# Window attention on one core: x in eight window-column transfers a block, weights loaded ahead of the statistics

## What is computed

```python
# x: (8, 56, 88, 192) float32; windows of 7 x 11 = 77 tokens, 8 heads of 24 channels
def _L0_conv_ref(x, qkv_w, qkv_b, proj_w, proj_b):
    xw = windows(x)                                   # (B*8*8, 77, 192)
    q, k, v = split(xw @ qkv_w + qkv_b, 3)            # per head 24 channels
    attn = softmax(einsum('bhnd,bhmd->bhnm', q, k) / sqrt(24))
    out = einsum('bhnm,bhmd->bhnd', attn, v)
    return unwindow(out @ proj_w + proj_b)
# _gn: group norm over (H, W, channels of a group), 32 groups of 6 channels, per image
x = x + _L0_conv_ref(_gn(x), qkv_w, qkv_b, proj_w, proj_b)
```

## Time and profile before

| | |
|---|---|
| median of three runs | 1518.98 us (1517.67 to 1539.47) |
| the profiled execution | 1531.71 us, span 1529.9 us |
| TensorE | 1361.8 us busy, 89% of the span |
| granted TensorE clock, mean | 0.971 |
| VectorE, ScalarE, GpSimd | 68%, 67%, 64% |
| DMA | 170.36 MB, mean 111 GB/s |

### The profile page before, as it was taken

The page is one execution under the profiler, slowest core; times in us unless marked ns, Lnnn a source line. Parts: engine busy times, 40 slices in busy tenths (PEclk is TensorE's granted clock), DMA queues, the critical chain, the costliest instruction groups (busy, mean ns, idle before and its releaser), DMA issues.

```text
span 1529.9 us, 84594 instructions
## 1 busy us (share of the span) xinstructions
PE 1361.8 (89%) x36832; PEld 1210.0 (79%) x36832; DVE 1047.8 (68%) x2227; ACT 1025.4 (67%) x1912; POOL 977.4 (64%) x1532
## 2 busy tenths in 40 slices
PE   0489899999998999999999989998999989999995
PEld 0377788888887888888888878887888878888884
DVE  5677677677766766777667866777667766666662
ACT  1567677766776677776767766776667666767761
POOL 0546766677665766767667776777667576767433
PEclk9999999999999999999999999999999999999997
DMA  7233344444444444444444443544433333433333
GB/s 211 69 95 88 112 114 129 120 118 124 108 128 100 115 129 104 129 107 132 111 114 134 113 108 108 132 123 116 116 99 97 98 95 89 106 95 93 85 84 105
DMA packets 129892, 170.36 MB, mean 111 GB/s; under 512 B 46898, under 2 KB 101490, under 8 KB 128628
## 3 DMA queue, kind: packets, MB, share of 16 engines
q1 hardware_dynamic: 98292, 100.59, 26.8%
q10 hardware_dynamic: 31232, 64.35, 14.0%
HBM read 132.04 MB, written 31.54 MB: 107 GB/s over the span
## 4 chain that ended last, share of the span: by engine, by line
PE 77%; DVE 8%; issue 6%; ACT 3%; POOL 3%; DMA 2%; SPq 1%; ACTq 0%; POOLq 0%; DVEq 0%
PE ps_a L698 13%; PE ps_b L698 13%; PE ps_q L698 11%; PE ps_k L698 11%; PE ps_a L731 10%; PE ps_s L744 8%; PE ps_s L758 5%; PE ps_k L826 4%; PE ps_q L793 3%; DVE neg_max L632 2%; POOL st_root L336 2%; DVE stat L495 2%; ACT probs L469 1%; DMA bias_in<-in_qkv_b 1%; DVE st_dev L510 1%
## 5 line engine op out<-in xcount | busy, mean ns | idle before, releaser
L632 DVE TENSOR_REDUCE neg_max<-ps_s 77x16 bf16<-77x1232 f32 x256 | 369.6, 1444 | 221.9 <-PE ps_s L758 221.1
L371 POOL TENSOR_TENSOR oT_lo<-o,oT_hi 128x308 f16<-128x308 f32 x256 | 193.7, 756 | 321.1 <-ACT oT_hi L463 321.1
L469 ACT ACTIVATE probs<-ps_s,exp_shift,exp_scale 77x1232 f32<-77x1232 f32 x256 | 349.2, 1364 | 9.9 <-PE ps_s L744 9.1
L731 PE MATMUL ps_a<-probs,v_all 77*32 77x77 f32 x8192 | 200.6, 234 | 41.1 <-issue 39.8
L452 ACT ACTIVATE v_all<-ps_a 77x384 f32<-77x384 f32 x256 | 124.9, 488 | 166.5 <-PE ps_a L698 166.4
L698 PE MATMUL ps_a<-wv_hiA,xT 128*128 128x192 f16 x1024 | 218.7, 253 | 2.5 <-issue 1.8
L345 POOL TENSOR_TENSOR o<-num,inv_all 128x308 f32<-128x308 f32 x256 | 216.2, 845 | 4.7 <-DMA inv_all<-den_dram 4.7
L439 ACT ACTIVATE xT<-ps_k 128x448 f16<-128x448 f16 x347 | 209.5, 642 | 8.9 <-PE ps_k L826 8.9
L731 PEld LDWEIGHTS ps_a<-probs,v_all 77*32 77x32 f32 x8192 | 148.7, 110 | 68.8 <-issue 44.4
L698 PE MATMUL ps_b<-wp_hi,oT_hi 128*112 128x192 f16 x694 | 188.1, 271 | 13.0 <-POOL oT_lo L371 6.8
L433 ACT ACTIVATE num<-ps_a 128x308 f32<-128x308 f32 x256 | 109.3, 427 | 133.0 <-PE ps_a L731 118.6
(11 more groups left out here) (148 smaller groups left out, 3854.9 us busy)
## 6 DMA issues: line engine op xcount, KB each, us to landing
inv_all<-den_dram SPq DMA_DIRECT2D x1024, 38.5 KB
x_stat<-in_x SPq DMA_DIRECT2D x24, 504.0 KB, 6.1
x_norm<-in_x ACTq DMA_DIRECT2D x32, 336.0 KB
x_norm<-in_x ACTq DMA_DIRECT2D x64, 168.0 KB
y_blk<-in_x SPq DMA_DIRECT2D x32, 336.0 KB
y_blk<-in_x SPq DMA_DIRECT2D x64, 168.0 KB
out<-y_blk ACTq DMA_DIRECT2D x32, 336.0 KB
out<-y_blk ACTq DMA_DIRECT2D x64, 168.0 KB
```

What stands on the lines that cost most here:

```text
L371: nc.gpsimd.tensor_tensor(oT_tokens(oT_lo, o), by_column(o32[o % 2]), oT_tokens(oT_hi, o), ALU.subtract).then_inc(pool_oT, 1)
L469: nc.scalar.activation(probs[i % 2][:, :, :].rearrange("p g (a n) -> p g a n", a=4), scores(), ACT.Exp, bias=exp_shift[0:TOK, :], scale=ex ...
L632: nc.vector.tensor_reduce(neg_max[:, :, :, HD:HD + 1].rearrange("p a g e -> p g (a e)"), scores(), AXIS.X, ALU.max, negate=True).then_inc( ...
L731: last = mm(o, v_all[s % V_BUFS][:, HEADS * w + NG * j + g, :], probs[s % 2][:, g, at:at + TOK], start=True, stop=True, skip_group_check=True)
```

## The change

x is loaded by window column: a block has eight transfers, each of 14 partitions by one contiguous row of 11 x 192 floats (8448 B), all eight on one semaphore per buffer. In the loop two are issued in each of the slots i with i + 19 = 8c + r, r = 0 to 3 (slots 5, 6, 7 and 0); before, one piece in each of slots 6, 0, 2, 4. A load of block c now waits for GpSimd to have split all of block c - 2. GpSimd waits once a block for all eight, and for block 1 it waits also for VectorE's third `normalise`.

In the prologue SP issues the two bias rows first, then proj_w, and bp last. ScalarE issues the first statistics half, waits for the six transfers of `dma_rows`, issues the second half and block 0, and issues block 1 only after its conversion of the weights. The pieces of y and of the output stay.

```diff
@@ semaphores
-        dma_x = [[sem(f"dma_x{p}_{k}") for k in range(len(PIECES))] for p in range(2)]
+        dma_x = [sem(f"dma_x{p}") for p in range(2)]
@@ SP
-            sp.dma_start(bp[:, :], proj_b.rearrange("(a c) -> a c", a=1).broadcast_to([128, CH])).then_inc(dma_w, 16)
             sp.wait_ge(pool_const, 2)
+            b_row = qkv_b.rearrange("(a c) -> a c", a=1)
+            for row in (CB, CB + ROW_G):
+                sp.dma_start(bias_in[row:row + 1, :], b_row).then_inc(dma_rows, 16)
             p_rows = proj_w.rearrange("(j g d) c -> g d j c", g=NG, d=HD)
             for g in range(NG):
                 sp.dma_start(p32[ROW_G * g:ROW_G * g + HD, :, :], p_rows[g, :, :, :]).then_inc(dma_rows, 16)
-            b_row = qkv_b.rearrange("(a c) -> a c", a=1)
-            for row in (CB, CB + ROW_G):
-                sp.dma_start(bias_in[row:row + 1, :], b_row).then_inc(dma_rows, 16)
+            sp.dma_start(bp[:, :], proj_b.rearrange("(a c) -> a c", a=1).broadcast_to([128, CH])).then_inc(dma_w, 16)
@@ GpSimd
-                    if n % PAIRS_IMG == 0 or n == PAIRS:
+                    if n == PAIRS:
+                        pool.wait_ge(dve_norm0, 3)
+                    if n % PAIRS_IMG == 0:
                         pool.wait_ge(stats_done, g + 1)
-                    if n % 2 == 0:
-                        pool.wait_ge(dma_x[parity(n)][n % PAIRS // 2], 16 * (n // PAIRS // 2 + 1))
+                    if n % PAIRS == 0:
+                        pool.wait_ge(dma_x[parity(n)], NWC * 16 * (n // PAIRS // 2 + 1))
@@ ScalarE
-            def load_x(c, k):
+            def load_x(c, w):
                 if c == 2:
-                    act.wait_ge(dve_x0, 2 * k + 2)
-                reach(act, pool_x, PAIRS * (c - 3) + 2 * k + 2)
-                nc.scalar.dma_start(piece(x_norm[c % 2], k), piece_of(x_blk, c, k)).then_inc(dma_x[c % 2][k], 16)
+                    act.wait_ge(dve_x0, PAIRS)
+                reach(act, pool_x, PAIRS * (c - 2))
+                nc.scalar.dma_start(x_norm[c % 2][ROWS * w:ROWS * (w + 1), :, :].rearrange("p c d -> p (c d)"), x_blk[c, w, :, :])\
+                    .then_inc(dma_x[c % 2], 16)
+
+            def load_block(c):
+                for w in range(NWC):
+                    load_x(c, w)
@@ ScalarE, prologue
             for h in range(2):
+                if h == 1:
+                    act.wait_ge(dma_rows, 6 * 16)
                 for n in range(2):
                     nc.scalar.dma_start(x_stat[h][:, n * TILES:(n + 1) * TILES, :].rearrange("p c d -> p (c d)"),
                                         x_rows[2 * h + n, :, :]).then_inc(dma_stat[h], 16)
-            for c in range(2):
-                for k in range(len(PIECES)):
-                    load_x(c, k)
+            load_block(0)
@@ ScalarE, behind the weight conversion
             nc.scalar.activation(wv["Bb"][low, :], bias_in[low, v], ACT.Copy).then_inc(act_w, 1)
+            load_block(1)
             act.wait_ge(stat_var, 1)
@@ ScalarE, main loop
-                c, r = divmod(i + 18, PAIRS)
-                if r % 2 == 0 and 2 <= c < BLOCKS:
-                    load_x(c, r // 2)
+                c, r = divmod(i + 19, PAIRS)
+                if r < 4 and 2 <= c < BLOCKS:
+                    load_x(c, 2 * r)
+                    load_x(c, 2 * r + 1)
@@ VectorE
-            dve.wait_ge(dma_x[0][0], 16)
+            dve.wait_ge(dma_x[0], NWC * 16)
             normalise(1, 0, 4)
-            dve.wait_ge(dma_x[0][1], 16)
             normalise(2, 4, 3)
             split_rest(0)
             split_rest(1)
-            dve.wait_ge(dma_x[0][2], 16)
-            dve.wait_ge(dma_x[0][3], 16)
             normalise(3, 7, 4)
```

## The result

| | median us | range | ratio to the kernel before, 95% interval |
|---|---|---|---|
| kernel before | 1519.0 | 1517.7 to 1539.5 (3 runs) | |
| changed kernel | 1544.8 | 1539.7 to 1545.0 (3 runs) | 1.017 (1.013 to 1.021) |
| changed kernel again, later session | 1539.6 | 1534.7 to 1548.3 (3 runs) | 1.003 (0.996 to 1.011) |

Every number here is of runs in the faster state; a fourth run of that later session, 1560.4 us at a granted clock of 0.956, was in the slower state, and with it the median would be 1544.0.

A forecast was written before the change was run, and what follows sets the result against it. TensorE, busy 89% of the span, was taken to bound the kernel after a DMA and VectorE start. Terms -8.4 - 1.7 + 3.5 - 3 = -9.6 us took the median from 1519.0 to 1509.4 us, range 1486 to 1527.

The forecast's parts named there:

- Gate: Prologue: VectorE's first reduction, waiting for the last weights and biases, moves from 21.7 to 13.3 us, -8.4 us.
- the gate only moves: Rival, chance 0.15: the second statistics half lands at 29.0 and stops VectorE for 5.4 of the 8.4 us; 1515 us.
- GpSimd's wait: First normalisation: GpSimd waits for VectorE's third normalisation, so VectorE runs undisturbed; -1.7 us (0 to -3.0).
- The 1.3 that I gave back for contention: First normalisation: part of the 3.0 us gain returned because GpSimd's operations now fall on VectorE's later splits.
- Issues of the loads: Loop, ScalarE: eight issues of x a block at 0.42 us each put 0.13 us on each slot 7, +3.5 us.
- 0.70 each: Rival, chance 0.08: each issue of x costs 0.70 us, lengthening slot 6 by 0.74 us, +20 us in all; 1526 us.
- The same bytes at other instants: Loop: moving x's loads to other slots flattens DMA traffic that delays instruction code; -3 us, near bounds 0 and -12.
- code arrives in time: Rival, chance 0.2: flatter traffic removes a third of the 106 us of stalls and lower clock, -35 us; 1477 us.
- it changes no term: the load is hidden either way: Loads of x: 14 rows should get 14 engines where pieces ran on 8; counted as no effect on time.
- part (c): Steady loop: TensorE's unexplained waits, 62 us, read as late instruction code; with lower clock, some 106 us touched by DMA traffic.
- code arrives later: Rival, chance 0.12: heavier traffic in slots 5 to 0 adds a quarter more stalls, +26 us; 1539 us, waits above 78.
- I am wrong if those waits move by more than 15: Failure test: TensorE's waits on "issue", 62 us before, moving by more than 15 us refutes the forecast.

The follow-up runs named there:

- experiment 8: Changed kernel with x loaded in four strided pieces in slots 5, 6, 7, 0 and y's pieces four slots later: 1480.4 us, ratio 0.964 to the kernel before.
- Experiment 9: Changed kernel with each window-column transfer writing partitions w, w + 8, ..., w + 104, not 14 neighbours (output wrong): 1514.1 us, ratio 0.983 to the kernel before.
- experiment 1: Changed kernel with x's loads back in four strided pieces in old slots 6, 0, 2, 4, new prologue kept: 1523.6 us, ratio 0.992 to the kernel before.
- experiment 2: Changed kernel with x loaded in four strided pieces in the new slots 5, 6, 7, 0: 1492.7 us, ratio 0.973 to the kernel before.
- experiment 7: Changed kernel, window columns kept, with y's four pieces loaded four slots later: 1508.8 us, ratio 0.982 to the kernel before.
- experiment 10: Changed kernel without loads of x in the loop, all computation kept: 1462.1 us, ratio 0.949 to the kernel before.
- experiment 4: Changed kernel with one transfer of x a block, 112 rows of 8448 B, in slot 5: 1518.5 us, ratio 0.988 to the kernel before.
- experiment 12: Changed kernel with strided pieces of x in old slots 6, 0, 2, 4 and y four slots later: 1537.1 us, ratio 0.996 to the kernel before.

## Why the prediction was wrong

**Gate, right.** 13.3 forecast, 13.32 measured: -8.4 us, from wB's landing time and the bytes left behind it. The statistics' second half was there in time (its reductions follow the first half's without a gap, at 23.57), so the rival "the gate only moves" fell.

**GpSimd's wait, right in sum.** The split of step 0 ended at 42.6, 4.0 us after its chain's start at 38.62 (4.2 forecast). The start gained 10.2 us where 8.4 + 1.7 = 10.1 were forecast. The 1.3 that I gave back for contention hid another cause: block 1, in columns and beside the statistics of image 1, landed only at 49.4 (the 19.43 us on the chain above), GpSimd began there, and its first split at 55.35 is what the chain goes through. In experiment 8, with pieces in time, GpSimd began at 45.1 and the first row maximum came at 61.9, hardly earlier: there the contention is on the chain, a copy of VectorE at 0.85 us for 0.20 and a subtraction at 0.99 for 0.34, together the 1.3. In the changed kernel the size came out right by luck.

**Issues of the loads, right in price.** 0.39 us each, so the rival "0.70 each" fell. The +3.5 us that I added for them was not measured by itself. Experiment 9, with 0.77 us an issue, is 31 us faster than the changed kernel, so they are hardly what made the loop longer.

**"The same bytes at other instants", -3 us: the step that failed.** It went wrong twice, in opposite directions. The loop became 23.2 us longer where +3.5 - 3 = +0.5 was forecast. The new slots are worth -31 us, not -3, if pieces go into them: experiment 1 to 2. That is the size my rival "code arrives in time" gave it (35). Why the new slots are better is open, as two of the four loads still meet a store. And the form costs 47 us in those slots (experiment 2 to the changed kernel), which I had put at nothing, in the sentence "it changes no term: the load is hidden either way". I had found the one fact from which it follows, that 14 engines would carry a column, and stopped there: I asked how many engines carry a column and not where they write. The load is hidden, but it holds DMA engines, and TensorE's instruction code comes later for it. That the long waits end when late code has come is what the ten waits above show; that they go with the load's form and place is what experiments 2, 7, 9 and 10 show; that code is late because the two share engines is my reading. I had even named this mechanism in part (c) and weighed only bytes in it, where the same 64.36 MB hold 16.5% against 14.0% of the engines' time. Of the 47 us, 31 went with the partitions in experiment 9, together with the wider spacing of the issues; what the rest is (twice as many transfers, longer packets, 14 engines for 8) is open.

**The rival on the other side** gave 1539 for "code arrives later", and 1544.8 came by its mechanism: more time in waits on "issue" (71.3 us for 62.0), its longest waits grown, slots 7 and 0 longer. I had given it 0.12. Its reasons were half right: y's large pieces beside x count for columns (experiment 7: -32 us), but its "rows of 8448 B come in one piece" do not (experiment 4), and the partitions, which it lacked, have their part in the 31 us of experiment 9.

**What the forecast's own tests said.** "I am wrong if those waits move by more than 15": they moved by 9, under the bound, and to 71.3, short of the 78 that I had asked for the second rival; the loop moved by 23, since the granted clock fell too. The test was set on too small a part of the mechanism.

## What to carry to other kernels

A transfer that no engine waits for can still have a price: here 23 to 83 us for the same loads of x. Read the waits on "issue" of the engine that sets the end and, for two forms of a transfer in the same place, the queue's share of engine time beside its bytes. In this kernel, loads split by bytes within all partitions were 47 us faster of some 1540 than bands of neighbouring partitions in the same slots. And try other places for a hidden load: the same bytes in other slots were worth 31 us for the pieces of x, and y four slots later 12 to 32 us with x in the new slots, but nothing with x in the old ones (experiment 12).

## What the runs showed of the hardware

Instruction code can come late while data moves: in the changed kernel it was absent for 9 us while others moved 1.3 MB, and all ten long waits of TensorE ended 2.5 to 3.2 us after the packet of code that followed such a gap. The sum of the waits, 20 to 73 us, depends on slots and forms of transfers that carry quite other data. In that kernel each of the ten has a stretch at 0.50 granted clock (1.2 GHz) with it or just behind it, so that it costs more than its own length. And with the engines held for the same share, 14 rows to each band of 14 neighbouring partitions moved at 142 GB/s, to 14 partitions 8 apart at 196.
